# A macaron block of attention and expert layers: the last unit's exps and everything behind them in two halves of its queries, the maxima of units 5 to 8 in quarters, and new places in the order

## What is computed

```python
def ffn(x):                                     # x: [4, 512, 128]
    q, k, v = x @ Wq, x @ Wk_c @ Wk, x @ Wv_c @ Wv        # 16 heads of 8, rotary on q and k
    a = softmax(q k^T / sqrt(8)); x1 = rmsnorm(x + (a v) @ Wo) * n1
    shared = swiglu(x1 @ W_shared_in) @ W_shared_out      # hidden size 256
    g = argmax of 2 group logits; w = softmax over the group's 4 experts * p(g), best 2 kept
    h = swiglu(x1 @ W1_shared)
    routed = sum_e (h @ W2_experts[e]) * w[:, e]          # 8 experts
    return rmsnorm(x1 + shared + routed) * n2

def attn(x):                                    # left 64 channels, 16 heads of 4
    return (softmax(q k^T / sqrt(8)) v) @ Wo^T + bo

x = x + 0.5 * ffn(layernorm(x))
x = x + attn(layernorm(x))
x = x + 0.5 * ffn(layernorm(x))
```

## Time and profile before

| | us |
|---|---|
| median of 3 executions | 874.33 (873.68 to 875.46) |
| the profiled execution | 874.73 |
| its span in the trace | 872.9 |
| TensorE busy in the span | 811.1 (93%) |
| VectorE busy | 673.0 (77%) |
| ScalarE busy | 497.3 (57%) |
| GpSimd busy | 332.5 (38%) |

### The profile page before, as it was taken

How to read it: one execution, slowest core, us unless ns; L and a number is a source line. 1 busy time by engine, 2 the same in 40 slices (tenths; PEclk the granted TensorE clock), 3 DMA queues, 4 the chain that set the end, 5 groups by cost and what they waited for, 6 DMA issues and landing times.

```text
span 872.9 us, 12671 instructions
## 1 busy us (share of the span) xinstructions
PE 811.1 (93%) x4144; PEld 294.9 (34%) x4144; DVE 673.0 (77%) x1296; ACT 497.3 (57%) x1042; POOL 332.5 (38%) x685
## 2 busy tenths in 40 slices
PE   3589999999999999999889999999999999999967
PEld 2133234433433332332313223233344343333333
DVE  5687998778759767876989998898987787682247
ACT  1045776356537645754777777767764575477320
POOL 2054325362543444345231613325153621522342
PEclk9578999999999999999999999999999999999989
DMA  3536232130120101010130331403311300000000
GB/s 103 154 85 148 73 63 54 27 72 3 46 32 1 39 11 32 6 43 12 21 76 6 76 77 39 101 16 92 59 39 36 83 10 1 4 13 3 1 12 13
DMA packets 27258, 38.92 MB, mean 45 GB/s; under 512 B 6949, under 2 KB 24965, under 8 KB 25573
## 3 DMA queue, kind: packets, MB, share of 16 engines
q1 hardware_dynamic: 25165, 36.39, 17.6%
q10 hardware_dynamic: 2028, 1.72, 0.8%
HBM read 28.01 MB, written 9.50 MB: 43 GB/s over the span
## 4 chain that ended last, share of the span: by engine, by line
PE 72%; DVE 18%; ACT 3%; issue 2%; DMA 2%; POOL 2%; ACTq 0%; POOLq 0%; SPq 0%; DVEq 0%
PE ps_out L682 17%; PE ps L668 14%; PE ps L649 13%; PE ps L744 11%; DVE maxes L820 11%; PE ps L729 6%; PE ps L631 2%; ACT probs L984 2%; PE ps L736 1%; PE ps L638 1%; DVE src L898 1%; PE ps L707 1%; DVE stats L779 1%; PE ps L720 1%; DVE src L791 1%
## 5 line engine op out<-in xcount | busy, mean ns | idle before, releaser
L984 ACT ACTIVATE probs<-ps 128x512 f32<-128x512 f32 x768 | 417.0, 597 | 249.3 <-PE ps L668 247.0
L820 DVE TENSOR_REDUCE maxes<-ps 128x1 f32<-128x512 f32 x768 | 482.9, 683 | 75.9 <-PE ps L649 74.2
L649 PE MATMUL ps<-k_aug,q_aug 72*128 72x512 bf16 (+1 forms) x768 | 259.6, 390 | 18.9 <-DMA k_aug<-ones_row 17.0
L668 PE MATMUL ps<-q_aug,k_aug 75*128 75x512 bf16 (+1 forms) x768 | 263.2, 383 | 5.3 <-DMA q_aug<-max_parts_rows 3.3
L682 PE MATMUL ps_out<-probs,v_aug 128*18 128x512 f32 x1536 | 203.1, 601 | 5.4 <-ACT probs L984 4.9
L649 PEld LDWEIGHTS ps<-k_aug,q_aug 72*128 72x128 bf16 (+1 forms) x768 | 66.0, 98 | 193.3 <-issue 123.3
L668 PEld LDWEIGHTS ps<-q_aug,k_aug 75*128 75x128 bf16 (+1 forms) x768 | 66.4, 97 | 149.9 <-issue 94.5
L744 PE MATMUL ps<-w,hidden 128*128 128x512 f32 x256 | 117.0, 596 | 0.0
L911 DVE TENSOR_TENSOR prod<-ps,gate 128x512 f32<-128x512 f32 x56 | 38.7, 692 | 58.3 <-PE ps L744 42.6
L1170 POOL TENSOR_TENSOR prod<-prod 128x512 f32<-128x512 f32 x28 | 35.5, 1268 | 97.0 <-DVE prod L911 93.8
L744 PEld LDWEIGHTS ps<-w,hidden 128*128 128x128 f32 x256 | 47.6, 190 | 51.3 <-issue 46.8
(11 more groups left out here) (121 smaller groups left out, 665.9 us busy)
## 6 DMA issues: line engine op xcount, KB each, us to landing
q_aug<-qk_parts SPq DMA_DIRECT2D x7, 1152.0 KB
k_aug<-qk_parts SPq DMA_DIRECT2D x21, 384.0 KB
qk_parts<-parts SPq DMA_DIRECT2D x45, 128.0 KB, 2.3
q_aug<-qk_parts SPq DMA_DIRECT2D x8, 288.0 KB
k_aug<-qk_parts SPq DMA_DIRECT2D x24, 96.0 KB
qk_parts<-parts SPq DMA_DIRECT2D x24, 64.0 KB, 2.0
q_aug<-qk_parts SPq DMA_DIRECT2D x12, 96.0 KB
k_aug<-qk_parts ACTq DMA_DIRECT2D x12, 96.0 KB
```

Source lines behind the costliest of these rows:

```text
L649: pe.matmul(bank(use[0]), q_aug[p0:p1, r, at, qt * 128:(qt + 1) * 128], k_aug[p0:p1, r, at, :], start=True, stop=True).then_inc(bank_full[ ...
L668: pe.matmul(bank(use[0]), k_aug[p0:p1, r, at, kt * 128:(kt + 1) * 128], q_aug[p0:p1, r, at, :], start=True, stop=True).then_inc(bank_full[ ...
L820: dve.tensor_reduce(maxes[:, u % 2, qt, h:h + 1], full(use[0]), AX.X, ALU.max)\
L984: act.activation(probs[:, step % P_RING, c, :], full(use[0]), ACT.Exp, scale=scale)\
```

## The change

The steps behind the scores of unit 11 (`LAST`) are doubled: steps with `u = 11` work on queries 0 to 255 (the first half) and steps with `u = 12` on queries 256 to 511 (the second half), `tiles_of` giving the tiles. Unit 11's exps run first for all heads of the first half and then for all heads of the second. One exp step still fills one bank and is one activation of 128x512, but holds two key tiles of 256 queries, from two matmuls of 256 columns. Unit 11's maxima, and those of units 5 to 8, go in four pieces. The tables of places, `MAX_LATE` and the holding times have new numbers, and the tables are now different for more of the units. Two further sets (`MAX_PAIRS`, `EXP_PAIRS`) are added but empty, so nothing runs in pairs.

```diff
+MAX_PAIRS = set()
+EXP_PAIRS = set()
-VECTOR_EXPERTS = {UNITS - 1}
+LAST = UNITS - 1
+VECTOR_EXPERTS = {LAST, LAST + 1}
-EARLY_UNITS = {0, 1}
+EARLY_UNITS = {0, 1, 5, 6, 7, 8, LAST}
+def tiles_of(u):
+    return range(TT) if u < LAST else range(TT // 2 * (u - LAST), TT // 2 * (u - LAST + 1))
...
-PREP_THIRD = {"norm_stats": [17], "norm_apply": [20], "x_transpose": [22], "qk_project": [24, 34],
+PREP_THIRD = {"norm_stats": [16], "norm_apply": [18], "x_transpose": [22], "qk_project": [24, 33],
...
+POST_LAST = {"heads_out": [37], "heads_transpose": [40], "out_project": [44], "rms_stats": [46], "rms_apply1": [47],
+             "x1_transpose": [48], "logits": [55], "mlp_up": [51, 55, 57, 59],
+             "router": [55, 56, 56, 59, 62, 63, 67, 68], "shared_out": [66], "expert": [69, 72, 74, 75]}
+POST_SECOND_HALF = {"heads_out": [2], "heads_transpose": [6], "out_project": [7], "rms_stats": [7],
...
-MAX_LATE = [39, 36, 23, 12, 16, 18, 22, 19, 17, 15, 17, 20, 22]
+MAX_LATE = [39, 33, 23, 14, 16, 18, 22, 24, 25, 21, 18, 18, 9]
...
+                    if u == LAST:
+
+                        qh, g, k2 = s // 8, s // 2 % 4, s % 2
+                        h = group_head(g, c)
...
+                        for i in range(2):
+                            kt = 2 * k2 + i
+                            mm = pe.matmul(bank(use[0])[:, i * 256:(i + 1) * 256], k_aug[0:p1, r, h, kt * 128:(kt + 1) * 128],
+                                           q_aug[0:p1, r, h, qh * 256:(qh + 1) * 256], start=True, stop=True)
+                        mm.then_inc(bank_full[use[0][0]], 1)
...
-                    for t in range(TT):
+                    for t in tiles:
```

More of the change, by code:

```diff
@@ L168 @@
-PREP_ATTN = {"norm_stats": [7], "norm_apply": [11], "x_transpose": [15], "qk_project": [18, 35],
-             "qk_split": [31, 38], "v_project": [19], "stack": [34, 55]}
-POST = {"heads_out": [3, 4], "heads_transpose": [8], "out_project": [10], "rms_stats": [12, 61], "rms_apply1": [15],
-        "x1_transpose": [19], "logits": [23], "mlp_up": [28, 28, 31, 35], "router": [26, 26, 32, 34, 34, 35, 38, 41],
-        "shared_out": [39], "expert": [43, 43, 47, 47, 50, 50, 52, 55], "rms_apply2": [64], "ffn_out": [67]}
@@ L174 @@
-POST_ATTN = {"heads_out": [3, 6], "heads_transpose": [11], "out_project": [15], "attn_out": [24]}
-POST_LAST_BUT_ONE = {"heads_out": [4, 4], "heads_transpose": [7], "out_project": [10], "rms_stats": [11, 73],
-                     "rms_apply1": [15], "x1_transpose": [18], "logits": [20], "mlp_up": [31, 36, 40, 43],
-                     "router": [20, 27, 29, 29, 31, 31, 36, 42], "shared_out": [48],
-                     "expert": [52, 56, 60, 60, 61, 63, 65, 66], "rms_apply2": [73], "ffn_out": [77]}
@@ L179, with take @@
-POST_LAST = {"heads_out": [3, 4], "heads_transpose": [7], "out_project": [8], "rms_stats": [10],
-             "rms_apply1": [10], "x1_transpose": [13], "logits": [15], "mlp_up": [14, 18, 23, 27],
-             "router": [17, 18, 18, 24, 26, 26, 28, 30], "shared_out": [28],
-             "expert": [36, 36, 37, 42, 43, 43, 48, 52]}
-MAX_LATE = [39, 36, 23, 12, 16, 18, 22, 19, 17, 15, 17, 20, 22]
+    def take(self, name, u, place):
+        run = max_run(u) if name == "max_scores" else exp_run(u) if name == "exp_scores" else 1
+        n = 2 if name in TWO_BANKS else run if name in HOLD else 0
+        taken = sorted(sorted(range(BANKS), key=lambda i: self.free_at[i])[:n])
+        uses = []
+        for i in taken:
+            self.free_at[i] = max(place * 10, self.free_at[i]) + HOLD[name]
+            signal = taken[0] if run > 1 else i
+            if signal == i:
+                self.signals[i] += 1
+            uses.append((i, self.filled[i], self.released[i], (signal, self.signals[signal])))
+            self.filled[i] += 1
+        for i, _, _, then in uses:
+            self.released[i] = then
+        return uses
@@ new lines @@
+POST_ATTN = {"heads_out": [3, 3], "heads_transpose": [11], "out_project": [15], "attn_out": [14]}
+POST_LAST_BUT_ONE = {"heads_out": [3, 3], "heads_transpose": [6], "out_project": [8], "rms_stats": [9, 55],
+                     "rms_apply1": [11], "x1_transpose": [16], "logits": [18], "mlp_up": [20, 23, 27, 31],
+                     "router": [23, 24, 27, 29, 29, 30, 32, 32], "shared_out": [34],
+                     "expert": [35, 39, 40, 42, 43, 47, 47, 50], "rms_apply2": [60], "ffn_out": [60]}
@@ L893, in _ @@
                     if u in VECTOR_EXPERTS:
-                        if t == half == 0:
+                        if t == tiles[0] and half == 0:
                             taken(dve, "shared_out", u)
@@ L983, in _ @@
                         act.wait_ge(out_done, step - P_RING + 1)
-                    act.activation(probs[:, step % P_RING, c, :], full(use[0]), ACT.Exp, scale=scale)\
+                    act.activation(probs[:, step % P_RING, c:c + exp_run(u), :], both(use), ACT.Exp, scale=scale)\
                        .then_inc(bank_free[use[0][0]], 1)
```

382 lines of the change are left out of this document (240 added, 142 removed).

## The result

Over five executions each, the changed kernel takes 883.06 us (878.89 to 890.01) and the kernel before 873.68 (873.17 to 875.46): ratio 1.011, interval 1.0061 to 1.016. The profiled execution took 883.06, its span is 881.3 us, 8.4 more than before. Forecast was 865.6, faster.

What follows compares the result with a forecast made beforehand. TensorE, busy 93% of the span, was taken as the bound, with ordering gains at tail, attention units and start: 872.9 - 4.2 - 2.5 - 2.0 = 864.2 span, plus 1.8 outside: 866.0, median 865.6; 8-in-10 range 858.5 to 872.

Steps and rivals of the forecast that it cites:

- The failed step: Units 5 to 8: extra stores and loads of maxima each block SP about 2 us, with nothing urgent behind.
- rival (d): Last unit's exps: 256-column matmuls don't run in half the time; at 0.22 each, 879.7; chance with a slower mix 0.08.
- the two signs of being wrong: TensorE idling 9.4 us or more in the attention units again, or a tail behind T over 37 us.
- T: End of the last weighing, forecast about 835.5: 825.4 + 3.65 + 5.2 + 0.2 + 1.0.
- Start: 50 to 130 us: unit 2's norm stall should shrink, perhaps the low clock too; -2, bounds +2 and -6.
- Attention units: Units 5 to 8, 410 to 540 us: quarters remove waits, later places move maxima out; -2.5, bounds +3 and -7.
- Tail: Last unit in halves: the span ends at T + 33.2, so 868.7 against 872.9, -4.2.
- the rival by which they stand there: Last unit's exps: weight loads unhidden, 128 x 0.097 = 12.4 us more, total 878.0; no chance of its own given.
- The stall foreseen at the copy of `x1T`: Tail, second half: ScalarE's copy waits behind the first half's last squares and VectorE's expert operations; done at T + 13.4.
- VectorE's wait for the first half's gates: Tail: gates at about T + 5.1, some two microseconds after TensorE and VectorE are ready for them.

Runs made afterwards that it cites:

- experiment 6: Changed kernel with the second `stack` place late again (56) for units 8 to 11 alone: 875.11 us, ratio 0.9989.
- 9: Changed kernel, but for units 9 to 11 only the first half of k's heads is copied into the stack: 875.48 us, ratio 0.9969.
- experiment 1: Changed kernel with the second places of `stack` put back to 56 and 88: 877.22 us, ratio 1.0021.
- experiment 13: Kernel before with one number changed, `MAX_LATE[1]` 33 for 36: 885.2 us, ratio 1.0064.
- experiment 14: Kernel before with the change's row `PREP_SECOND`, but its second `stack` at 88 as before: 879.32 us, ratio 1.0025.
- experiment 7: Experiment 3's kernel plus maxima of units 5 to 8 in quarters and `MAX_LATE` 24, 25, 21 for units 7 to 9: 877.63 us, ratio 0.9999.
- experiment 3: Kernel before with the last unit in halves, last `MAX_LATE` 9, new step places behind units 10 and 11, and changed holding times: 874.16 us, ratio 0.9984.
- experiment 5: Changed kernel with second `stack` at 56 and 88, and `PREP_SECOND`, `PREP_THIRD`, `MAX_LATE` of units 1, 3, 10, 11 as before: 871.85 us, ratio 0.9956.
- 8: Experiment 3's kernel with the holding times (`HOLD`) as before: 872.24 us, ratio 0.9963.
- 15: Experiment 5's kernel with the holding times of before: 874.34 us, ratio 0.9953.

## Why the prediction was wrong, by its own steps

**The failed step** is the one sentence on SP in the paragraph on units 5 to 8, "their stores and loads on SP each block it for about 2 us, with nothing urgent behind", and with it that moved `stack` steps got no price at all. The 2 us were read where a store finds empty DMA engines. The table rows that moved 1.2 MB of k ahead of the store were in the diff, eight and five places up, and their size in the trace: three loads of 384 KB. That order alone costs 8.4 us in units 9 to 11 (experiments 6 and 9), and with the place 83 about 2 us at the start (unit 0 ends at 116.40 in experiment 1, 118.45 in the changed kernel). It was also the missing rival for slower: the rival (d) had its price on TensorE, where nothing was wrong. Nor did either of the two signs of being wrong appear: TensorE idled 9.0 us from 410 to 540, under the 9.4 named, and the tail behind T took 32.2 us, under 37.

**Start: -2 forecast, +6.1 measured.** The wait for unit 2's norm at 71.7 went, as forecast; it had next to no worth, for what comes next is bound by the landing of unit 1's k, 10 to 12 us behind its issue in six kernels. Nine of the kernels have TensorE wait for it until 86 to 90 us. In the kernel before the granted clock was 0.75 from 75 to 85, and TensorE came there late enough not to wait. Getting there earlier makes a wait (experiment 13), and the new `PREP_SECOND` delays k besides (experiment 14). The bound of +2 on this term was too small because it held only the stall that was seen.

**Attention units: -2.5 forecast, -4.0 seen at unit 7's end, 0 to 2 kept.** The waits for `max_parts_rows` in units 5 and 6 are gone and the size at that place is nearly right. But the text had itself said that six maxima leave this stretch "into the ffn stretch behind", and booked the departure and not the arrival. In that stretch TensorE is the bound (128.5 of 130 us busy from 570 to 700 before), so whatever arrives there is paid in full (experiment 7: 2.6 won, 2.8 lost). Of the 4.0, 1.4 come with other new tables of these units, which no run takes apart.

**Tail: -4.2 forecast, right.** The last weighing starts at 848.15 and ends at about 849.1; from there to the end are 32.2 us against 33.2 forecast and 47.5 before. It ends later than 835.5 mostly by what had been lost ahead. In experiment 3, where little was, it ends near 838.6, 3 us late, 1.6 of them lost ahead of unit 9. The other half is an addition that came out small: 3.4 us more ahead of unit 10's end (201.6 us from unit 7's end against 198.2) and 8.3 behind it (67.2 to T against 58.9), 11.7 for 10.1 forecast. Most of the 3.4 is only moved there: 11 of the last unit's maxima, 2.4 us of TensorE, run ahead of unit 10's end and no longer behind it (9 there, 20 before). Of the 1.6 us too little, two more transposes of maxima are 0.5, and new stalls are 1.3 where 1.0 was put: behind unit 10's end TensorE idles 2.1 us for 0.8 before, nearly all of it for the last exps of each half (0.98 us at 782.26, 0.96 at 837.65). The rest is not taken apart. Behind T it saved 15.3 us (32.2 for 47.5), 14.3 forecast, so the two errors nearly cancel: 11.7 - 15.3 is -3.6. The stall foreseen at the copy of `x1T` stands at 861.58 with 2.35 us. VectorE's wait for the first half's gates was 0.89 us, not two:

```profile
852.55 1.51 DVE L1021 SCALAR_TENSOR_TENSOR src<-ps,gate,src 128x128 f32<-128x128 f32 x4 [0.89 <-POOL gate L1301]
...
870.86 4.61 DVE L1021 SCALAR_TENSOR_TENSOR src<-ps,gate,src 128x128 f32<-128x128 f32 x12 [0.55 <-POOL gate L1301]
...
878.99 0.29 DVE L1052 TENSOR_TENSOR X<-X,src 128x128 f32<-128x128 f32 x1
```

**Rival (d), the 256-column exps, is refuted.** Four of them fit from 804.50 to 804.94, 0.11 us each, weight load included. TensorE at 63.97 of 65 us busy leaves no place for loads in the open, so the rival by which they stand there falls too. That the measured 883.06 lies nearest to these two rivals (879.7, 878.0) is coincidence.

**The parts together**, against before: start +6.1; attention 4.0 less and 2.8 more, -1.2; k ahead of the stores in units 9 to 11, +8.4; last unit with its earlier maxima, 7.4 less and 3.4 more, -4.0. The sum is +9.3 against 8.4 measured. The 0.9 too much lies between kernels that differ in more tables than these: from unit 4's end to unit 10's experiment 6 takes 350.3 us and experiment 3 takes 352.3, so the quarters, their places and the other new tables together keep 2.0 there, where the sum has 1.2.

**The version that wins** is the tail without the moved loads: 0.9956 (experiment 5), 0.9963 (8) and 0.9953 (15). That is 0.4 to 0.5% under the kernel before, where the tail term alone stood for 0.48%. But two more kernels have the same tail and loads and are not clear of 1: 0.9984 (experiment 3) and 0.9999 (7). What sets them apart from the three is not shown.

## What to carry to other kernels

When a hand-made order moves a step, list what it issues on every queue, and price the small transfer that now goes behind a big one by the big one's time in flight, not by its own; here another queue didn't help, fewer bytes or another order did. Work pushed out of one stretch must be booked where it arrives: a gain read at the end of a stretch isn't one until the next milestone confirms it. And a wait that vanishes is worth nothing when what comes next is bound by another thing; ask what lands when. A forecast's signs of being wrong should also watch the terms that it priced at nothing.
